# Decoder layer on one core: the bf16 parts of the softmax maxima moved from VectorE to GpSimd, with two places of the schedule shifted

## The reference, cut to what matters

```python
x = _layernorm(x + _L0_attn_ref(x, ...))
x = _layernorm(x + _L0_xattn_ref(x, ctx_1024, ctx_1024, mask, ...))
x = _layernorm(x + _L0_ffn_ref(x, ...))

attn = jnp.einsum('bhqd,bhkd->bhqk', q, k) * scale
attn = jax.nn.softmax(jnp.where(causal, -jnp.inf, attn), axis=-1)
out = jnp.einsum('bhqk,bhkd->bhqd', attn, v) @ w_proj.T
```

## Time and profile before

| | us |
|---|---|
| median of 3 runs | 953.13 (951.49 to 953.75) |
| the profiled execution, its own time | 952.55 |
| its span in the trace | 950.8 |
| TensorE busy | 852.0 (90% of the span) |
| VectorE, ScalarE, GpSimd busy | 720.1, 632.8, 538.7 |
| granted TensorE clock, mean | 0.969 of full speed |

### The profile page before, as it was taken

One profiled execution on the slowest core, in us unless ns is written; L12 is line 12 of the kernel. 1 busy time (PEld: TensorE's weight loads), 2 busy tenths in 40 slices (PEclk: granted clock), 3 DMA queues, 4 the chain that ended last, 5 costly groups with the idle time before them and its releaser, 6 DMA issues.

```text
span 950.8 us, 21384 instructions
## 1 busy us (share of the span) xinstructions
PE 852.0 (90%) x7381; PEld 649.0 (68%) x7381; DVE 720.1 (76%) x1765; ACT 632.8 (67%) x1404; POOL 538.7 (57%) x1047
## 2 busy tenths in 40 slices
PE   3367898999999999999999999999999999889887
PEld 2235565776867677776867676776867676657677
DVE  7788787787888878877888878877888879675522
ACT  1132453787878787787878778787878777776352
POOL 7554464656656574665756575655756665444143
PEclk8769898999999999999999999999999999999999
DMA  3794382845656382736676482826566472823101
GB/s 113 105 179 82 50 108 37 115 48 91 80 102 79 60 111 47 108 41 109 74 102 79 71 104 46 109 37 116 66 102 79 74 97 46 105 34 54 27 2 34
DMA packets 79660, 74.21 MB, mean 78 GB/s; under 512 B 8608, under 2 KB 78912, under 8 KB 79552
## 3 DMA queue, kind: packets, MB, share of 16 engines
q1 hardware_dynamic: 75024, 68.11, 50.7%
q10 hardware_dynamic: 4528, 4.73, 1.9%
HBM read 17.49 MB, written 4.20 MB: 23 GB/s over the span
## 4 chain that ended last, share of the span: by engine, by line
PE 60%; DVE 21%; ACT 5%; issue 5%; POOL 4%; DMA 3%; SPq 0%; ACTq 0%; POOLq 0%; DVEq 0%
PE bank L401 56%; DVE mx L1048 8%; PE bank L428 3%; POOL pr L1433 3%; DVE qn L1179 2%; ACT pr L854 2%; DVE x L1135 2%; ACT bank L788 1%; DMA stk2k<-nat1k 1%; POOL rstd L1412 1%; DVE y L1107 1%; DVE nt L1169 1%; ACT nat2q L788 1%; DVE rest L1022 1%; DVE st L1114 1%
## 5 line engine op out<-in xcount | busy, mean ns | idle before, releaser
L1433 POOL TENSOR_SCALAR_AFFINE_SELECT pr<-pr 128x256 f32<-128x256 f32 x512 | 223.1, 445 | 201.8 <-ACT pr L854 199.7
L854 ACT ACTIVATE pr<-bank 128x384 f32<-128x384 f32 x512 | 239.0, 495 | 138.2 <-PE bank L401 136.9
L1048 DVE TENSOR_REDUCE mx<-bank 128x3 f32<-128x384 f32 x512 | 264.5, 549 | 75.3 <-PE bank L401 70.6
L788 ACT ACTIVATE bank<-cmaskb 128x384 f32<-128x384 bf16 x331 | 155.0, 491 | 37.9 <-DVE mx L1048 33.0
L401 PE MATMUL bank<-w,g 128*128 128x256 f32 x576 | 171.2, 388 | 0.3 <-ACT g L874 0.3
L401 PE MATMUL bank<-stk2k,stk2q 97*128 97x128 bf16 (+1 forms) x512 | 87.2, 254 | 13.3 <-ACT bank L788 13.3
L401 PEld LDWEIGHTS bank<-w,g 128*128 128x128 f32 x576 | 89.3, 190 | 3.9 <-ACT g L874 0.7
L401 PE MATMUL bank<-stk1q,stk1k 100*128 100x256 bf16 (+1 forms) x512 | 79.2, 251 | 5.2 <-ACT pr L854 3.6
L874 ACT ACTIVATE g<-bank,b 128x256 f32<-128x256 f32 x144 | 65.1, 467 | 22.9 <-PE bank L401 22.9
L401 PE MATMUL bank<-stk1k,stk1q 97*128 97x128 bf16 (+1 forms) x512 | 75.4, 247 | 0.3 <-ACT bank L788 0.3
L401 PE MATMUL bank<-cmaskb,idb 128*128 128x256 bf16 x181 | 52.1, 288 | 25.0 <-DMA stk2k<-nat1k 13.9
(11 more groups left out here) (171 smaller groups left out, 1842.0 us busy)
## 6 DMA issues: line engine op xcount, KB each, us to landing
stk1q<-nat1q SPq DMA_DIRECT2D x90, 128.0 KB, 4.6
stk1k<-nat1k SPq DMA_DIRECT2D x90, 128.0 KB, 5.3
stk2k<-nat2k SPq DMA_DIRECT2D x90, 128.0 KB, 4.3
stk2q<-nat2q SPq DMA_DIRECT2D x90, 128.0 KB, 5.6
xT<-in_xT SPq DMA_DIRECT2D x16, 256.0 KB, 5.4
ctxT<-in_ctxT SPq DMA_DIRECT2D x16, 256.0 KB, 5.8
x<-in_x SPq DMA_DIRECT2D x16, 256.0 KB, 6.0
out_x<-x SPq DMA_DIRECT2D x15, 256.0 KB, 2.2
```

The costliest lines, as they stand in the source:

```text
L788: return nc.scalar.activation(out, in_, ACT.Copy)
L854: nc.scalar.activation(pr[:, h % (2 * HG), :], ring_bank("T", a, b, h)[:, 0:3 * P], ACT.Exp, scale=HD ** -0.5)\
L1048: V.tensor_reduce(mx3[:, h, :], scored[:, 0:3 * P].rearrange("p (k t) -> p k t", k=3), AX.X, ALU.max, negate=True).then_inc(s_mx[a], 1)
L1433: G.affine_select(out=slot, in_=slot, compare_op=ALU.is_ge, fill=0.0, base=0, pattern=[[0, 2], [1, P]], channel_multiplier=-1).then_inc(s_ ...
```

## The change

VectorE still makes `nm`. The four operations that split it into bf16 parts are issued by GpSimd, with a semaphore of their own between them. For self attention they stand in GpSimd's step after `x2b` and ahead of the power of x2; for cross attention they stand between mask 1 and mask 2 of T1 (`PARTS2_AT = 2`). `mx3` becomes one tile for each attention. `out_proj(1, s)` goes from head 9 of T2 to head 7, where it stands ahead of `values(2, c, 0)`; the power of x1 goes from ahead of mask 13 of T2 to ahead of mask 12. `RSTD1_LAST`, for the last sequence, stays.

```diff
-        mx3 = sb("mx3", [P, H, 3])
+        mx3 = [None] + [sb(f"mx3{a}", [P, H, 3]) for a in (1, 2)]
...
             def maxima(a, b, between):
+                wait(dve, s_nm[a], b)
                 for h in range(H):
...
-                    V.tensor_reduce(mx3[:, h, :], scored[:, 0:3 * P].rearrange("p (k t) -> p k t", k=3),
+                    V.tensor_reduce(mx3[a][:, h, :], scored[:, 0:3 * P].rearrange("p (k t) -> p k t", k=3),
                                     AX.X, ALU.max, negate=True).then_inc(s_mx[a], 1)
 
             def max_parts(a, b):
                 dve.wait_ge(s_mx[a], H * (b + 1))
-                V.tensor_copy(nm[a][:, 0, :], mx3[:, :, 0])
-                V.tensor_tensor(nm[a][:, 1, :], mx3[:, :, 1], mx3[:, :, 2], ALU.min).then_inc(s_nm[a], 1)
-                dve.wait_ge(s_nm[a], 4 * b + 1)
-
-                wait(dve, s_mt[a], b)
-                V.tensor_copy(mp[a][:, :, 0, :], nm[a][:, :, :]).then_inc(s_nm[a], 1)
-                dve.wait_ge(s_nm[a], 4 * b + 2)
-                V.tensor_tensor(nr[a][:, :, :], nm[a][:, :, :], mp[a][:, :, 0, :], ALU.subtract).then_inc(s_nm[a], 1)
-                dve.wait_ge(s_nm[a], 4 * b + 3)
-                V.tensor_copy(mp[a][:, :, 1, :], nr[a][:, :, :]).then_inc(s_nm[a], 1)
-                dve.wait_ge(s_nm[a], 4 * b + 4)
-                V.tensor_tensor(mp[a][:, :, 2, :], nr[a][:, :, :], mp[a][:, :, 1, :], ALU.subtract).then_inc(s_mp[a], 1)
+                wait(dve, s_mp[a], b)
+                V.tensor_copy(nm[a][:, 0, :], mx3[a][:, :, 0])
+                V.tensor_tensor(nm[a][:, 1, :], mx3[a][:, :, 1], mx3[a][:, :, 2], ALU.min).then_inc(s_nm[a], 1)
...
+            def max_parts(a, b):
+
+                n = 3 * b
+                pool.wait_ge(s_nm[a], b + 1)
+                wait(pool, s_mt[a], b)
+                G.tensor_copy(mp[a][:, :, 0, :], nm[a][:, :, :]).then_inc(s_part[a], 1)
+                pool.wait_ge(s_part[a], n + 1)
+                G.tensor_tensor(nr[a][:, :, :], nm[a][:, :, :], mp[a][:, :, 0, :], ALU.subtract).then_inc(s_part[a], 1)
+                pool.wait_ge(s_part[a], n + 2)
+                G.tensor_copy(mp[a][:, :, 1, :], nr[a][:, :, :]).then_inc(s_part[a], 1)
+                pool.wait_ge(s_part[a], n + 3)
+                G.tensor_tensor(mp[a][:, :, 2, :], nr[a][:, :, :], mp[a][:, :, 1, :], ALU.subtract).then_inc(s_mp[a], 1)
...
+                if live(s):
+                    max_parts(1, s)
                 if live(f):
                     inverse_deviation(2, f)
                     inverse_norm2(f)
...
-                    mask_probs(1, s, {})
+                    mask_probs(1, s, {PARTS2_AT: lambda: max_parts(2, c)} if live(c) else {})
+                elif live(c):
+                    max_parts(2, c)
...
-K2_AT, OUT1_AT, QK1_AT, V1_AT = 1, (3, 9), (3, 6), 13
+K2_AT, OUT1_AT, QK1_AT, V1_AT = 1, (3, 7), (3, 6), 13
...
+PARTS2_AT = 2
-RSTD3_AT, RSTD1_AT, RSTD1_LAST = 3, 13, 10
+RSTD3_AT, RSTD1_AT, RSTD1_LAST = 3, 12, 10
```

More of the change, by code:

```diff
@@ L169, in build @@
         s_split = two("split_ready"); s_stk = two("stack_loaded")
-        s_bias = two("bias_written"); s_s = two("scores_ready"); s_mx = two("max_ready"); s_nm = two("dve_nm"); s_mp = two("maxparts_ready")
+        s_bias = two("bias_written"); s_s = two("scores_ready"); s_mx = two("max_ready"); s_nm = two("dve_nm"); s_part = two("maxparts_step"); s_mp = two("maxparts_ready")
         s_mt = two("maxT_ready"); s_mT = two("maxT_copied"); s_ml = two("max_loaded")
```

## The result

| | before | after |
|---|---|---|
| median, us | 953.06 (951.49 to 953.75, 4 runs) | 963.15 (961.42 to 964.8, 4 runs) |
| span of the profiled execution | 950.8 | 963.1 |
| VectorE, GpSimd busy | 720.1, 538.7 | 706.9, 563.1 |

The ratio is 1.0108, with a 95% interval of 1.0086 to 1.013: 10.1 us slower, where 961.5 us was forecast. The profiled execution is the slowest of the four after (964.8). The page first: the chain that ended last, against the earlier trace rows.

A forecast was written before the change was run, and what follows sets the result against it. The last-ending chain was read as 60% TensorE, 21% VectorE, 4% GpSimd. To 952.55 us came +8.4 (cross parts), +0.45 (first step), +0.75 (S1) and -0.5 (last sequence): +9.1, 961.6, stated as 961.5 us; range 947 to 968, its own 957 to 966.

The forecast's parts named there:

- The wait at the parts: Head 5 of T1: TensorE waits 0.56 us for cross parts behind mask 1 on GpSimd, 15 steps, +8.4 us.
- The low end: Cross parts in T1: four GpSimd operations of 0.221 us, 1.12 us in all, making TensorE's wait 0.34 us.
- Self parts in S2: Parts on GpSimd have 0.40 us to spare before TensorE; later power of x2 costs nothing; first step once +0.45 us.
- VectorE's relief: VectorE gives up 0.98 us in T1 and 0.89 in S2, worth nothing because it then waits for TensorE.
- The power alone: End of T2: power of x1 one mask sooner brings power, VectorE's tail and next S1 0.63 us sooner.
- The two T2 edits undo each other: Projection at head 7 makes value product 1 and mask 11 0.63 us late, so VectorE waits for the power as before.
- The residual in S1: TensorE enters S1 0.63 us late with x1 on time; 0.05 us left per step (0 to 0.3), +0.75 us.
- The last sequence: VectorE waits on the self projection itself there; its sooner place may give 0.5 us once.
- The lock on the port: T1: first cast held until `xn` ends, parts 0.25 us later, 965 us; 979 with small operations high; chance 0.12.
- The rival that the burst costs nothing: T2: value product 1 not held, power's 0.63 us kept against 0.56 of new wait, about 951.5 us; chance 0.13.
- The faster rival: Power's advance in T2 exceeds the wait at head 5 of T1: 948 us, or 943 without wait; chance 0.22.
- The other signs of being right: VectorE idle about 1.5 us ahead of `mT`, 1.5 or more ahead of `x`; steps 0.6 us longer.

The follow-up runs named there:

- experiment 2: The changed kernel with power of x1 back at mask 13 and self projection back at head 9, only the parts on GpSimd: 958.7 us against 953.34, ratio 1.0063.
- experiment 5: The changed kernel with the self projection at head 8 of T2 in place of head 7: 950.71 us against 951.62 for the kernel before, ratio 0.9981.
- experiment 6: The changed kernel with the self projection at head 9 only in the last two steps with both attentions live: 960.15 us, ratio 1.0075 to the kernel before.
- experiment 1: The kernel before with only the power of x1 moved from mask 13 to mask 12 of T2: 946.9 us against 953.34, ratio 0.9941.
- 7: The kernel before with only the power of x1 moved ahead of mask 11 of T2: 950.03 us against 951.62, ratio 0.9971.
- Experiment 8: The kernel before with the power of x1 at mask 11 and the self projection at head 8: 946.74 us against 951.62, ratio 0.9938.
- experiment 3: The kernel before with the power of x1 at mask 12 and projection at head 7, parts left on VectorE: 959.68 us against 953.34, ratio 1.0071.

## Why the prediction was right, and where it was not

**The wait at the parts: right in place and cause, too large.** The sum had 0.56 us a step; the runs show 0.31. From the end of mask 1 to TensorE's start are 1.20 us (430.61 to 431.81), where I had 1.44. The straight lines between GpSimd's rows gave 0.244 for a copy and 0.305 for two inputs; medians are 0.212 and 0.247. (The row of 0.221 that stood in for a small copy is a TENSOR_SCALAR.) And the 0.05 us for a start behind the mask doesn't exist. The low end, 0.34, was almost exact. The waits of the whole trace check experiment 2: 12 new ones of 0.31 us, 0.32 at the first self parts (forecast +0.45), and 0.21, 0.31, 0.31 and 0.47 at the four other cross parts, where TensorE had waited for VectorE before. Their sum is 5.3 us; measured were 5.4. The term stood at 8.4 + 0.45.

**Self parts in S2: right.** They run from 418.41 to 419.56, TensorE's transposes follow at 420.19 with only their 0.16 us of issue, and the later power of x2 shows no reader that waits.

**VectorE's relief: right.** Nothing came of 13 us less work.

**The power alone: right in `x`, one step short.** The forecast was 0.63 us a step; `x` came 0.65 sooner and 0.19 were given back. The sentence that failed is that the tail and the next S1 "come 0.63 us sooner". It moved masks past VectorE's Newton steps and didn't price the meeting.

**The two T2 edits undo each other: right.** Value product 1, mask 11 and `x` stand where the working put them, to 0.03 us, and experiment 5 shows the threshold between a burst of three heads and one of four. `y` is sooner by 1.23 us, not 1.4; the prediction's own times for the projection's end, 444.38 and 443.14, give 1.24.

**The residual in S1: 0.05 forecast, 0.14 measured.** It was laid to TensorE's lateness. Most of it is the same meeting of masks and Newton steps: with `x` on time, the way to the first maximum takes 2.57 us instead of 2.40. The edit also acts in fewer steps than the 15 of the sum, since the last sequence keeps its own place for the power. The kernel before shows the size within itself, in the timelines of VectorE and GpSimd:

```profile
449.43 0.21 DVE L1167 TENSOR_TENSOR nt<-rr 128x64 f32<-128x64 f32 x1
449.58 0.41 POOL L1433 TENSOR_SCALAR_AFFINE_SELECT pr<-pr 128x256 f32<-128x256 f32 x1 [0.22 <-ACT pr L854]
449.68 0.39 DVE L1169 SCALAR_TENSOR_TENSOR nt<-ms,nt 128x64 f32<-128x64 f32 x1
450.62 0.23 DVE L1169 SCALAR_TENSOR_TENSOR nt<-ms,nt 128x64 f32<-128x64 f32 x1
```

The same operation takes 0.39 us beside the mask of 449.58 to 449.99, and 0.23 with GpSimd at rest. The Trainium skill (SBUF — State Buffer, Who interferes with whom) says that a VectorE operation with two SBUF inputs contends with a GpSimd one that reads SBUF; the trace agrees: this one ends at 450.06, 0.08 us behind the mask, and in all 26 cases of the kernel before in which it begins inside a mask with more than 0.1 us of it left, it ends 0.073 to 0.078 us behind.

**The last sequence: wrong in sign.** The forecast had -0.5 us. "The projection's operand was ready ahead of head 6" was read from one steady step, where two q/k projections give VectorE the time to make it. Without them the projection waits 1.68 and 0.71 us. That is about 3 us in the times (experiment 6) and 4.5 in the profile, 1.62 of them a fall of the clock.

**The lock on the port: it acts, at a fifth of the rival's price.** Here are the two instructions of `xn` by themselves, which the row above has merged; the first begins inside mask 1 (430.20 to 430.61) and the cast (430.56) inside the first:

```profile
430.25 0.51 DVE L1136 TENSOR_SCALAR xn<-x,rr 128x256 f32<-128x256 f32 x1
...
430.68 0.34 DVE L1136 TENSOR_SCALAR xn<-x,rr 128x256 f32<-128x256 f32 x1
```

The first is held by the mask and takes 0.51 us for 0.34; it ends 0.145 us behind the mask. The cast takes 0.26 us for 0.21 and ends 0.07 us behind that first instruction. So it was held for 0.05 us until one instruction had ended, not for 0.25 until both had; that was the rival's slip, and the 0.05 are inside the 0.31. By the exclusive lock in that section of the Trainium skill, which the prediction cites, whoever starts first blocks the other for the whole instruction, and the trace agrees: in all 33 cases of the changed kernel in which an instruction of `x` begins inside a mask with more than 0.1 us of it left, it ends 0.145 to 0.147 us behind that mask. The prediction's "no more than 0.07 us" was read from the masks alone. The rival that the burst costs nothing falls with value product 1. The faster rival's condition was half met: no advance of the power was left to set against the wait.

The other signs of being right are there too: VectorE idles 1.12 us ahead of `mT` (1.5 forecast) and 1.46 ahead of `x` (1.5), and a step is 0.45 us longer (0.6).

So the direction and the steady step rest on the mechanism, but that the total is right to 1.7 us is luck, since errors of opposite sign met: the parts were 3.5 us too dear (8.85 for 5.3), the residual some 1.2 too cheap (13 steps of 0.09), and the end 3.5 or more too cheap. What stays open is the start: the profile is 2.8 us late by 220 us, of which the four sets of parts that had waited by then explain 1.2 (0.32 + 0.21 + 0.31 + 0.31), and an execution's start varies by as much.

The kernels with a sooner power lose 1.4 and 2.2 us after 805 us (experiments 1 and 7). Their traces show where: the granted clock falls twice in each, and not once in the kernel before between 170 and 950 us. A window around the second fall of each, first experiment 1, then 7, with the columns as above:

```profile
914.00:919.00 5.00, 3.92 (x19) 3.52 (x20) 1.37 (x4) 2.60 (x8) 0.00 (x0) 0.66 0.01 2
881.00:885.00 4.00, 4.00 (x24) 3.57 (x24) 1.68 (x4) 0.95 (x2) 3.35 (x9) 0.57 0.00 0
```

Lateness grows by 1.02 and 1.56 us across them, and by 0.95 and 0.85 from 842 to 873 us, where each has a first fall (0.66 from 846 to 851 us). Experiment 8 has no such fall after 170 us until its last microseconds, and loses nothing from 805 us on. What sets these falls off isn't shown.

## What to carry to other kernels

Moving work to an engine with spare time moves it behind that engine's queue: what counts is what stands ahead of it there and when its reader comes, not the engine's busy share. The parts cost 5.4 us behind two masks, and no steady step lost anything with them ahead of the masks. Two edits that each pay can cancel when both use the slack of one deadline, so find the step in the schedule (here three heads or four) and stay on the near side of it. Read the first and the last steps too: a pipeline that drains has lost the work that covered a wait.

## What the runs showed of the hardware

A GpSimd operation on 128 x 32 elements took 0.212 us as a cast and 0.247 with two inputs, about the 0.221 and 0.239 of two columns (a TENSOR_SCALAR and a two-input operation); a straight line up to the next larger row is too steep there. The same idle of 1.68 us on TensorE was followed by a granted clock of 0.56 in one execution and by no fall in another (experiment 3), so the idle alone doesn't decide it; where it came, it cost about 1.6 us. Other falls of the clock late in an execution cost 1.02 us (experiment 1), 1.56 (7) and 1.55 (3), and not every kernel here has one; they have to be taken out before the end of a single profile is read as the cost of a schedule.

A VectorE operation that begins inside a GpSimd mask isn't shown as waiting: the hold counts as its own duration, and the sign of it is an end at a fixed distance behind the mask's, 0.145 us for the 128 x 256 TENSOR_SCALAR of `x` and 0.076 for the 128 x 64 operations of a Newton step with two inputs.
